# Two-layer language-model tower: the first layer's experts write whole rows back to three tables instead of adding into one

## The reference, cut to what matters

```
Sm = softmax(xf @ W_router + b_router)                 # (16384, 32)
G_ek, idx_ek = top_k(Sm.T, 512)                        # per expert: 512 tokens and their gates
up  = einsum('gjkh,ghf->gjkf', xf[idx_ek], W_up) + b_up     # F = 341, W_up shared by 4 experts
Eout = einsum('ekf,efh->ekh', silu(up), W_down) + b_down
y = zeros.at[idx_ek].add(G_ek[..., None] * Eout)       # a token may be picked by many experts
h = h + y
h = h + attention(layernorm(h)) ; h = h + top2_experts(layernorm(h))
```

## Time and profile before

| | us |
|---|---|
| median of 3 runs | 2603.01 |
| lowest, highest | 2602.21, 2605.15 |
| the profiled execution's own time | 2606.08 |
| its span (first to last instruction) | 2604.4 |
| mean granted PE clock | 0.935 of full |

### The profile page before, as it was taken

One profiled execution on the slowest core, in us unless ns is written; L12 is line 12 of the kernel. 1 busy time (PEld: TensorE's weight loads), 2 busy tenths in 40 slices (PEclk: granted clock), 3 DMA queues, 4 the chain that ended last, 5 costly groups with the idle time before them and its releaser, 6 DMA issues.

```text
span 2604.4 us, 59053 instructions
## 1 busy us (share of the span) xinstructions
PE 2278.5 (87%) x16671; PEld 2037.5 (78%) x16687; DVE 1839.4 (71%) x8212; ACT 1687.3 (65%) x5272; POOL 1549.7 (60%) x1870
## 2 busy tenths in 40 slices
PE   4999887666766599999999999999999999999865
PEld 4887765455555499999999999999999888988854
DVE  4887756644443378888888888778778888888622
ACT  3787653222222477777777788888888777877643
POOL 6445100688888568888888874444444665466453
PEclk9999989777777799999999999999999999999977
DMA  2333200344444521111111136555555776476687
GB/s 81 101 91 98 84 22 1 65 73 73 74 76 77 106 60 35 33 34 36 31 36 33 34 101 164 159 153 158 157 141 161 215 208 192 114 231 190 175 250 237
DMA packets 304259, 283.98 MB, mean 109 GB/s; under 512 B 33931, under 2 KB 252651, under 8 KB 303936
## 3 DMA queue, kind: packets, MB, share of 16 engines
q1 hardware_dynamic: 254144, 211.15, 29.6%
q0 software_dynamic: 46336, 61.16, 10.2%
q10 hardware_dynamic: 3456, 7.89, 1.0%
HBM read 185.85 MB, written 88.43 MB: 105 GB/s over the span
## 4 chain that ended last, share of the span: by engine, by line
PE 53%; POOL 16%; DVE 14%; issue 9%; DMA 4%; ACT 2%; SPq 1%; POOLq 0%; DVEq 0%; ACTq 0%
POOL hbuf L839 7%; PE bank L2065 7%; PE bank L2155 6%; PE bank L2141 6%; PE bank L2076 5%; PE bank L2064 4%; PE bank L2108 4%; PE bank L2088 4%; PE bank L2116 4%; PE bank L2090 3%; PE bank L2089 3%; POOL xe L831 3%; POOL vo_place L758 2%; PE bank L1948 1%; DVE pr_place L1581 1%
## 5 line engine op out<-in xcount | busy, mean ns | idle before, releaser
L888 POOL DMA_INDIRECT zbuf<-pc,kb x248 | 249.2, 1005 | 268.2 <-DVE pc L1743 212.1
L873 POOL DMA_INDIRECT spread_rows<-kb,pos x256 | 255.8, 999 | 173.9 <-DVE pc L1743 83.8
L1090 ACT ACTIVATE pr_place<-bank,nmax 128x128 f32<-128x128 f32 x512 | 188.8, 369 | 193.4 <-DVE nmax L1561 192.7
L2065 PE MATMUL bank<-xT,gT 128*128 128x256 f32 x1024 | 307.8, 383 | 0.0
L1581 DVE COPY pr_place<-bank 128x384 f32<-128x384 f32 x512 | 281.5, 550 | 9.2 <-PE bank L2076 8.3
L2155 PE MATMUL bank<-wvo_part,x_part 128*128 128x512 f32 x768 | 270.3, 460 | 0.0
L1560 DVE TENSOR_REDUCE nmax<-bank 128x1 f32<-128x128 f32 x512 | 143.9, 281 | 175.5 <-PE bank L2065 170.7
L1100 ACT ACTIVATE bank<-causal 128x384 f32<-128x384 f32 x512 | 253.5, 495 | 19.7 <-PE bank L2199 3.6
L2076 PE MATMUL bank<-ident,pr_place 128*128 128x128 f32 x1536 | 252.0, 273 | 15.8 <-DVE pr_place L1581 15.5
L2076 PEld LDWEIGHTS bank<-ident,pr_place 128*128 128x128 f32 x1536 | 196.5, 140 | 83.6 <-DVE pr_place L1574 20.3
L2141 PE MATMUL bank<-x_part,wqk_part 128*128 128x256 f32 x1536 | 245.6, 296 | 1.2 <-DVE x_part L1688 1.2
(11 more groups left out here) (336 smaller groups left out, 6556.2 us busy)
## 6 DMA issues: line engine op xcount, KB each, us to landing
pa<-bundle SPq DMA_DIRECT2D x198, 321.0 KB
wu_more<-bundle SPq DMA_DIRECT2D x66, 321.0 KB
junk<-zbuf SPq DMA_DIRECT2D x32, 512.0 KB
kb<-spread_rows SPq DMA_DIRECT2D x248, 65.0 KB
xrow<-xr SPq DMA_DIRECT2D x32, 320.0 KB, 2.4
hbuf<-h SPq DMA_DIRECT2D x32, 256.0 KB, 3.2
hx<-hbuf SPq DMA_DIRECT2D x64, 128.0 KB
h3buf<-h SPq DMA_DIRECT2D x64, 128.0 KB
```

The costliest lines, as they stand in the source:

```text
L873: pool.indirect_dma_start(out=spread_rows, out_offset=bass.IndirectOffsetOnAxis(ap=pos[:, k, j:j + 1], axis=0), in_=xr4s[g % 2][:, k, j], ...
L888: pool.indirect_dma_start(out=zbuf, out_offset=bass.IndirectOffsetOnAxis(ap=xu_at(t)[:, C + 1:XW].bitcast(U32), axis=0), in_=yu[:, t % YR] ...
L2065: pe.matmul(s2[:, P:3 * P], g[:, P:2 * P], xT3[:, p], start=False, stop=True, skip_group_check=True)\
```

## The change

The tables `hbuf` and `xrow` become three equal tables with 288 floats a row: normalised row (128), probabilities (32), sum (128). Both layouts lie together in one SBUF tile, `rows4` (four groups of rows).
- First layer: `h1` and `xr` are parts of `rows4[:, g % 4]`. SP stores the whole tile three times, once to each table, after the probabilities are there (six DMAs of 576 KB a round); the stores at L584 are gone. DVE waits ahead of L1327 for the stores of the group four back; ScalarE's wait for stores is gone.
- Experts: expert e works on table b = e % 3. `take` gathers whole rows of 288 floats into `rows4[:, b]`. DVE's `weigh` adds the gated output to the sum part of the gathered rows, in four pieces of 128 rows (for table 2 the gate is negated). `give` writes the whole rows back with plain scatters, each as soon as its piece is there. A table is gathered again three experts later, after its scatters have landed; the wait for the expert before is gone. GpSimd's order is now `take(e+1)`, `give(e)`.
- PE turns the rows of e just ahead of its up-projection (no longer those of e+1 ahead of the down-projection of e), does `bases(e+3)` between the second and third part of the up-projection, and splits the down-projection over banks 4 and 7; ahead of its second piece it waits for `oneh` of e+3, and ahead of piece c for DVE's piece c-2.
- Second layer: SP loads three parts a block. GpSimd forms `hx` = part 0 + part 1 at h = 5 (`sum_first`) and minus part 2 at h = 6 (`sum_rest`), two blocks ahead, four additions of 128x128 a block. Tables 0 and 1 hold h1 plus their experts' outputs, table 2 holds h1 minus them, so that the result is h1 plus all.

```diff
+ROWA = ROW + C
+NTAB = 3
...
-        hbuf = nc.dram_tensor("hbuf", (NTOK, C), F32).ap()
-        xrow = nc.dram_tensor("xrow", (NTOK, ROW), F32).ap()
+        tables = [nc.dram_tensor(f"table{k}", (NTOK, ROWA), F32).ap() for k in range(NTAB)]
-        hbuf_b = hbuf.rearrange("(n j p) c -> n p j c", j=2, p=P)
+        sums_b = [t[:, ROW:ROWA].rearrange("(n j p) c -> n p j c", j=2, p=P) for t in tables]
...
-        h1 = sb("h1", [P, 2, TG, C])
-        xr = sb("xr", [P, 2, TG, ROW])
+        rows4 = sb("rows4", [P, 4, TG, ROWA])
+
+        def h1_at(g):
+            return rows4[:, g % 4, :, ROW:ROWA]
+
+        def x2_at(g):
+            return rows4[:, g % 4, :, 0:C]
...
+        def down_at(c):
+            return bank[7 if c % 2 else 4][:, (c // 2) * P:(c // 2 + 1) * P]
...
+        hparts = rows4[:].rearrange("p k j c -> p (k j c)")[:, 0:2 * NTAB * 2 * C].rearrange("p (q k j c) -> p q k j c", q=2, k=NTAB, j=2)
...
             def store_rows(g, p):
                 sp.wait_ge(p_ready, g + 1)
-                sp.dma_start(xrow_g[bass.ds(g, 1)].rearrange("a p j c -> (a p) j c"), xr[:, p]).then_inc(stored_x[p], 16)
+                for k in range(NTAB):
+                    sp.dma_start(tables_g[k][bass.ds(g, 1)].rearrange("a p j c -> (a p) j c"), rows4[:, g % 4]).then_inc(stored_x[p], 16)
...
-                for p in range(2):
-                    g = 2 * i + p
-                    sp.wait_ge(h1_ready, g + 1)
-                    sp.dma_start(hbuf_g[bass.ds(g, 1)].rearrange("a p j c -> (a p) j c"), h1[:, p]).then_inc(stored[p], 16)
...
             def load_h2(n, p):
-                sp.dma_start(hx[:, p], hbuf_b[bass.ds(n, 1)].rearrange("a p j c -> (a p) j c")).then_inc(h2_in[p], 16)
-
-            for p in range(2):
-                sp.wait_ge(added[p], 64 * (E0 // 2))
+                for k in range(NTAB):
+                    sp.dma_start(hparts[:, p, k], sums_b[k][bass.ds(n, 1)].rearrange("a p j c -> (a p) j c")).then_inc(h2_in[p], 16)
+
+            for b in range(NTAB):
+                sp.wait_ge(written[b], 64 * len(range(b, E0, NTAB)))
...
-            def take(e, q):
-
-                p = q % 2
+            def take(e):
+                b = e % NTAB
                 pool.wait_ge(idx_ready, e + 1)
+                if e >= NTAB:
+                    pool.wait_ge(written[b], 64 * (e // NTAB))
                 pool.nop(nofuse=True)
                 for c in range(TG):
-                    pool.indirect_dma_start(out=xe[:, p, c], out_offset=None, in_=xrow,
-                                            in_offset=bass.IndirectOffsetOnAxis(ap=idx[:, q, c:c + 1], axis=0))\
-                        .then_inc(xe_in[p], 16)
-
-            def give(e, p, q):
-                pool.wait_ge(ye_ready, e + 1)
-                pool.nop(nofuse=True)
+                    pool.indirect_dma_start(out=rows4[:, b, c], out_offset=None, in_=tables[b],
+                                            in_offset=bass.IndirectOffsetOnAxis(ap=idx[:, e % 4, c:c + 1], axis=0))\
+                        .then_inc(xe_in[e % 2], 16)
+
+            def give(e):
+                b = e % NTAB
                 for c in range(TG):
-                    pool.indirect_dma_start(out=hbuf, out_offset=bass.IndirectOffsetOnAxis(ap=idx[:, q, c:c + 1], axis=0),
-                                            in_=ye[:, p, c], in_offset=None, compute_op=ALU.add).then_inc(added[p], 16)
+                    pool.wait_ge(ye_ready, TG * e + c + 1)
+                    pool.nop(nofuse=True)
+                    pool.indirect_dma_start(out=tables[b], out_offset=bass.IndirectOffsetOnAxis(ap=idx[:, e % 4, c:c + 1], axis=0),
+                                            in_=rows4[:, b, c], in_offset=None).then_inc(written[b], 16)
 
             for p in range(2):
-                pool.wait_ge(stored[p], 16 * NP)
-                pool.wait_ge(stored_x[p], 16 * NP)
-            take(0, 0)
-            take(1, 1)
-
-            def serve(v, last):
-                for q in range(4):
-                    e, p = 4 * v + q, q % 2
-                    if not (last and q >= 2):
-                        take(e + 2, (q + 2) % 4)
-                    if not (first(v) and q == 0):
-
-                        n = 2 * v + (q + 1) // 2 if q % 2 else 2 * v + q // 2
-                        pool.wait_ge(added[1 - p], 64 * n)
-                    give(e, p, q)
-            serve(0, False)
-            for v in range(1, NU - 1):
-                serve(v, False)
-            serve(NU - 1, True)
-            for p in range(2):
-                pool.wait_ge(added[p], 64 * (E0 // 2))
+                pool.wait_ge(stored_x[p], 16 * NTAB * NP)
+            take(0)
+            for e in range(E0):
+                if e + 1 < E0:
+                    take(e + 1)
+                give(e)
+            for b in range(NTAB):
+                pool.wait_ge(written[b], 64 * len(range(b, E0, NTAB)))
...
             def residual(n):
                 i, p = n // 2, n % 2
-                pool.wait_ge(h2_in[p], 16 * (i + 1))
+                pool.wait_ge(h2_ready, 2 * n + 2)
...
+            def sum_first(n):
+                pool.wait_ge(h2_in[n % 2], 16 * NTAB * (n // 2 + 1))
+                for j in range(2):
+                    ins = pool.tensor_tensor(hx[:, n % 2, j], hparts[:, n % 2, 0, j], hparts[:, n % 2, 1, j], ALU.add)
+                ins.then_inc(h2_ready, 1)
+
+            def sum_rest(n):
+                pool.wait_ge(h2_ready, 2 * n + 1)
+                for j in range(2):
+                    ins = pool.tensor_tensor(hx[:, n % 2, j], hx[:, n % 2, j], hparts[:, n % 2, 2, j], ALU.subtract)
+                ins.then_inc(h2_ready, 1)
+
+            for n in range(2):
+                sum_first(n)
+                sum_rest(n)
...
+                if h == 5 and n + 2 < NB:
+                    sum_first(n + 2)
+                if h == 6 and n + 2 < NB:
+                    sum_rest(n + 2)
...
             def second_norm(g, p, i):
-                if not isinstance(g, int) or g >= 2:
-                    act.wait_ge(stored_x[p], 16 * i)
-                normalise(xr[:, p], h1[:, p], p).then_inc(x2_ready, 1)
+                normalise(x2_at(g), h1_at(g), p).then_inc(x2_ready, 1)
...
                     dve.wait_ge(y_mm, g0 + p + 1)
-                    if rear:
-                        dve.wait_ge(stored[p], 16 * i)
-                        dve.wait_ge(x2_ready, r0 + p + 1)
-                    dve.tensor_tensor(h1[:, p], bank[4 * p + 2][:, :].rearrange("p (j c) -> p j c", j=TG), xg_at(g0 + p), ALU.add)\
+                    if i >= 2:
+                        dve.wait_ge(stored_x[p], 16 * NTAB * (i - 1))
+                    dve.tensor_tensor(h1_at(g0 + p), bank[4 * p + 2][:, :].rearrange("p (j c) -> p j c", j=TG), xg_at(g0 + p), ALU.add)\
...
-                if guard is not None:
-                    dve.wait_ge(added[q % 2], guard)
+                if e >= 4:
+                    dve.wait_ge(written[(e - 4) % NTAB], 64 * ((e - 4) // NTAB + 1))
...
-            def gates(e, p, n, guard):
-
-                dve.wait_ge(xe_in[p], guard)
-                if not isinstance(e, int) or e >= 2:
-                    dve.wait_ge(ye_ready, e - 1)
-                n.done(dve.tensor_copy(gate[:, p], xe[:, p, :, bass.ds(C + e, 1)].rearrange("p c a -> p (c a)")))
+            def gates(e, p, n):
+                b = e % NTAB
+                dve.wait_ge(xe_in[p], 64 * (e // 2 + 1))
+                if e >= 2:
+                    dve.wait_ge(ye_ready, TG * (e - 1))
+                sign = -1.0 if b == 2 else 1.0
+                n.done(dve.tensor_scalar(gate[:, p], rows4[:, b, :, bass.ds(C + e, 1)].rearrange("p c a -> p (c a)"), sign, None, ALU.mult))
                 n.wait()
 
             def weigh(e, p):
-
-                dve.wait_ge(dn_mm, e + 1)
-                dve.tensor_tensor(ye[:, p], bank[4][:, :].rearrange("p (c h) -> p c h", c=TG),
-                                  gate[:, p].unsqueeze(2).to_broadcast([P, TG, C]), ALU.mult).then_inc(ye_ready, 1)
+                for c in range(TG):
+                    acc = rows4[:, e % NTAB, c, ROW:ROWA]
+                    dve.wait_ge(dn_mm, TG * e + c + 1)
+                    dve.scalar_tensor_tensor(out=acc, in0=down_at(c), scalar=gate[:, p, c:c + 1], in1=acc,
+                                             op0=ALU.mult, op1=ALU.add).then_inc(ye_ready, 1)
...
-                dve.wait_ge(h2_in[p], 16 * (i + 1))
+                dve.wait_ge(h2_ready, 2 * n + 2)
...
-            def turn_rows(e, p, guard):
-                pe.wait_ge(xe_in[p], guard)
+            def turn_rows(e):
+                pe.wait_ge(xe_in[e % 2], 64 * (e // 2 + 1))
                 for c in range(TG):
-                    ins = pe.transpose(bank[0][:, c * P:(c + 1) * P], xe[:, p, c, 0:C], ident[:])
+                    ins = pe.transpose(bank[0][:, c * P:(c + 1) * P], rows4[:, e % NTAB, c, 0:C], ident[:])
                 ins.then_inc(xeT_mm, 1)
-            turn_rows(0, 0, 64)
 
```

(21 more changed lines are left out.)

40 lines of the change are left out of this document (16 added, 24 removed).

## The result

| | before | after |
|---|---|---|
| median, us | 2602.61 (8 runs) | 2611.9 (8 runs) |
| profiled execution, its span | 2606.08, 2604.4 | 2610.73, 2609.0 |
| first statistics of the attention (block 0) | 879.8 | 838.6 |
| block 0 to block 30 | 599.9 | 627.8 |
| block 30 to block 63 | 913.2 | 935.0 |

What follows compares the result with a forecast made beforehand. GpSimd's issuing was taken to bound the experts, a chain of waits the first layer; in the attention TensorE is 99% busy. -63.2 + 8 + 6 = -49 us gave 2557, on the runs' scale 2554; range 2528 to 2600.

Steps and rivals of the forecast that it cites:

- First layer, +8 us: First layer: larger stores make each round's last gather land 0.6 us late in 13 rounds; ends 0 and +30.
- Rival 2: First layer: stores of three tables hold GpSimd's gathers, +118 in place of +8, 2664 us; chance 0.10.
- Scatter of 1.03 us: Experts: a plain scatter of 1152-byte rows takes 1.03 us, ends 0.96 and 1.58; the adding one took 1.58.
- Rival 3: Experts: a plain scatter stays as dear as the adding one, 12.6 us an expert, +64, 2618 us; chance 0.05.
- Start of the attention, +3.1: Attention's start: two more loads of 0.45 us and four additions of 0.46 with hand-overs for the first block, +3.1 us.
- 10.5 us an expert, -66.3 us up to SP's load: Experts: GpSimd's issue takes 10.4 us an expert, 10.5 with slow stretches; SP's load, now at 877.7, comes after 811.4.
- the long idle time that precedes each fall goes: Experts: TensorE's idle times get shorter (longest about 2.8 us), the argument against a halved clock in each down-projection.
- The way round through TensorE: Experts: TensorE's steps in a row take 8.9 us at full clock, 1.5 us under GpSimd's 10.4, so GpSimd stays bound.
- rival 1: Experts: TensorE's row of steps at a mixed clock becomes the bound, 11.6 us an expert, +33, 2587 us; chance 0.17.
- Attention, +6 us: Attention: GpSimd's additions, 1.85 us more in each of 64 blocks, cost 0.1 us a block; ends 0 and +30.
- the additions fit in, with 0.7 us to spare: Attention: GpSimd waits 2.5 us a block for VectorE, against 1.85 us of additions.
- Rival 4: Attention: GpSimd has no room for the additions, +0.5 us in each block, +30, 2584 us; chance 0.09.

Runs made afterwards that it cites:

- experiment 9: Kernel before, plus two stores of 1152-byte rows per first-layer group to tables nothing reads: 2603.8 us, ratio 1.0015 (2713.8, 1.0019 on a slower chip).
- c2_busy: Changed kernel plus two 128x512 products an expert on TensorE, ahead of the turns, result overwritten: 2585.4 us, ratio 0.9951 to the kernel before.
- f2_no_sums: Changed kernel without GpSimd's sums, attention loading one table only, on a chip where the kernel before takes 2600 us: 2555.2 us, ratio 0.9819.
- a1_no_sums: Same kernel as f2_no_sums, on a chip where the kernel before takes 2707 to 2709 us: 2709.8 us, ratio 1.0006.

## Why the prediction failed, step by step

- **First layer, +8 us:** 8.4 (first take 459.2 to 467.6). Right in size, in part by luck: experiment 9 bears out 3 us of its cause. Rival 2 did not come. The one row that spoke for it, a gather issued 2.04 us late, was misread as the stores' doing: the same 2.04 us stand ahead of the same gather, the 114th of 128, in all kernels here, with three times the stores' traffic too (at 260.22 in the changed one).
- **Scatter of 1.03 us:** 0.98. Rival 3 did not come. **Start of the attention, +3.1:** 3.2 (from SP's load to the first statistics 5.2 us, 2.1 before).
- **10.5 us an expert, -66.3 us up to SP's load** (to which the start's +3.1 was added): from first take to SP's load 418.5 us became 365.8, -52.7, that is 13.6 short. The first scatters of experts 0 to 30 are 11.0 us apart in the mean, which makes 15.6; a shorter first and last expert give 2 back. The step that failed is the sentence "the long idle time that precedes each fall goes". The way round through TensorE was counted at 8.9 us at the full clock, and is 8.7 in every second expert. But the rows then land 2.65 us after TensorE is ready for them, this idle time is followed by the lower clock, and the expert takes 11 to 12.7 us. That is rival 1 in half of the experts. c2_busy, which fills the idle time, gives 20 us back in this stage.
- **Attention, +6 us:** +27.9 and +21.8 up to block 63, less 3.9 in the tail, 46 in all. The failed step is "the additions fit in, with 0.7 us to spare". It counted GpSimd's spare time, and said of VectorE only that it "has 17% idle". Rival 4 named the place (+0.5 a block, 30 us) but the wrong engine: what ran out was not GpSimd's time but VectorE's, which is held in its two-input instructions and its divisions until GpSimd's own is all but over: VectorE is busy 431.6 us instead of 408.1 in blocks 6 to 30, and they last 515.1 instead of 491.3. The rule was to be had (the Trainium skill, SBUF — State Buffer, Who interferes with whom), and the prediction passed over it; to apply it, it needed only the kinds of VectorE's instructions in slots 5 and 6.

Sum by these terms, on spans, with unrounded terms: 2604.4 + 8.4 - 52.7 + 3.2 + 45.8 = 2609.0.

## What to carry to other kernels

Before work is put on GpSimd "because it has time", look at what VectorE runs beside it: here its subtraction with two SBUF inputs and its divisions in SBUF waited for GpSimd's additions, and the same additions were cheaper on VectorE itself, in slots in which it waits for another engine. If a change shortens the waits of a stage by putting TensorE's steps in a row, look for the idle time that is left ahead of the largest product; here the lower clock followed it. Time such a change on more than one chip where its margin is small.

## What the runs showed of the hardware

- A VectorE instruction on 128x4 numbers takes 0.16 us when it starts 0.52 us into a GpSimd division of 0.92 and 0.63 when it starts 0.19 into it; a division of 128x128 0.27 alone, 1.11 beside a scatter and two additions, 1.46 beside a scatter and two fills.
- Two products of 128x512 an expert for nothing made the kernel 23 us faster (granted clock 0.89 to 0.99).
- One program takes 2600 us on some chips and 2708 on others, and a change worth 1.8% on the one (f2_no_sums) is worth nothing on the other (a1_no_sums), where late hand-overs from TensorE add up to 48 us in the experts.
